# Laying every engine's instruction list a second time, by when each step can begin, in a four-layer fp32-accurate transformer kernel

## The reference

```
L0: mod = silu(c) @ w_adaln + b;  x += g1 * attention(modulate(ln(x)));  x += g2 * moe(modulate(ln(x)))   # 4 experts, top 2
L1: the same form with a plain MLP, and attention among the 16 heads of one token:
    softmax(einsum('nthd,ntkd->nthk', q * scale, k)), then einsum('nthk,ntkd->nthd', attn, v)
L2: attention over tokens, plain MLP
L3: U = qr(P).Q;  R = expm(skew(silu(cond) @ W.T + b));  x + ((x @ U) @ R - x @ U) @ U.T
```

## Time and profile before

| | |
|---|---|
| median of 3 runs | 1548.58 us (1545.59 to 1550.38) |
| profiled execution, its own time | 1545.17 us |
| its span, first to last instruction | 1543.1 us |
| mean granted TensorE clock | 0.952 of full |
| instructions | 30439 |
| busy: TensorE, VectorE, ScalarE, GpSimd | 1367.0, 950.9, 818.6, 397.8 us |
| DMA | 91.82 MB, mean 60 GB/s |

### The profile page before, as it was taken

The page is one execution under the profiler, slowest core; times in us unless marked ns, Lnnn a source line. Parts: engine busy times, 40 slices in busy tenths (PEclk is TensorE's granted clock), DMA queues, the critical chain, the costliest instruction groups (busy, mean ns, idle before and its releaser), DMA issues.

```text
span 1543.1 us, 30439 instructions
## 1 busy us (share of the span) xinstructions
PE 1367.0 (89%) x11841; PEld 822.0 (53%) x11841; DVE 950.9 (62%) x2315; ACT 818.6 (53%) x1597; POOL 397.8 (26%) x571
## 2 busy tenths in 40 slices
PE   4667999897999989999899988788899989998988
PEld 2333555563655545655466554455465556555655
DVE  5666877746567555555465555766777866656453
ACT  2555655657566424653345433675555665654542
POOL 1122232213233221222231322232332423321110
PEclk9887999998999999999999999899999999998998
DMA  5122234452213120321113122230000120000010
GB/s 154 48 65 92 83 102 136 149 158 86 65 43 104 38 76 8 75 80 62 51 24 96 44 75 83 51 67 13 17 9 5 36 74 13 5 7 13 1 39 31
DMA packets 76740, 91.82 MB, mean 60 GB/s; under 512 B 38989, under 2 KB 69814, under 8 KB 73270
## 3 DMA queue, kind: packets, MB, share of 16 engines
q1 hardware_dynamic: 74486, 87.52, 19.6%
q10 hardware_dynamic: 2112, 2.36, 0.5%
HBM read 73.22 MB, written 16.38 MB: 58 GB/s over the span
## 4 chain that ended last, share of the span: by engine, by line
PE 60%; DVE 13%; issue 10%; ACT 5%; DMA 5%; POOL 4%; SPq 2%; DVEq 0%; POOLq 0%; ACTq 0%
PE P L1346 27%; PE P L1506 4%; PE P L1508 4%; PE P L1507 4%; PE P L1475 3%; DVE NM L1776 3%; PE P L1466 2%; PE P L1373 2%; PE P L1442 2%; PE P L1523 1%; POOL N L2225 1%; PE P L1363 1%; POOL X L2210 1%; PE P L1517 1%; DVE AT L1908 1%
## 5 line engine op out<-in xcount | busy, mean ns | idle before, releaser
L1346 PE MATMUL P<-XT,W 128*128 128x512 f16 x1512 | 355.5, 387 | 6.1 <-DVE NM L1776 2.6
L2210 POOL TENSOR_TENSOR X<-X,TM 128x288 f32<-128x288 f32 x144 | 122.0, 847 | 660.3 <-DVE TM L1851 438.8
L1506 PE MATMUL P<-W,H 128*128 128x288 f16 x864 | 252.9, 293 | 1.1 <-DVE H L1845 1.0
L1507 PE MATMUL P<-W,H 128*128 128x288 f16 x864 | 252.4, 292 | 0.0
L1508 PE MATMUL P<-W,H 128*128 128x288 f16 x864 | 252.3, 292 | 0.0
L1346 PEld LDWEIGHTS P<-XT,W 128*128 128x128 f16 x1512 | 143.8, 99 | 180.5 <-issue 21.3
L2118 ACT ACTIVATE ARENA<-P 128x512 f32<-128x512 f32 x256 | 136.7, 596 | 122.7 <-PE P L1466 122.2
L2128 ACT ACTIVATE G<-P 128x512 f32<-128x512 f32 x216 | 128.4, 594 | 126.9 <-PE P L1346 115.8
L1776 DVE TENSOR_REDUCE NM<-P 128x2 f16<-128x512 f32 x256 | 159.8, 686 | 3.5 <-PE P L1451 2.9
L1845 DVE TENSOR_TENSOR H<-G,H 128x512 f16<-128x512 f32 x138 | 98.9, 719 | 82.0 <-ACT H L2129 81.5
L1346 PE MATMUL P<-WQ,XT 128*128 128x288 f16 x1008 | 143.6, 294 | 1.5 <-DVE NM L1776 0.9
(11 more groups left out here) (307 smaller groups left out, 2232.1 us busy)
## 6 DMA issues: line engine op xcount, KB each, us to landing
W<-scr_w SPq DMA_DIRECT2D x9, 1440.0 KB, 6.0
W<-scr_w SPq DMA_DIRECT2D x9, 1368.0 KB, 5.9
scr_w<-W SPq DMA_DIRECT2D x4, 1440.0 KB, 6.4
scr_w<-W SPq DMA_DIRECT2D x4, 1368.0 KB, 5.7
STG<-in_L_w SPq DMA_DIRECT2D x8, 576.0 KB, 4.3
STG<-in_L_w SPq DMA_DIRECT2D x9, 432.0 KB, 4.1
STG<-in_L_WT SPq DMA_DIRECT2D x11, 324.0 KB, 4.2
G<-scr_ada SPq DMA_DIRECT2D x24, 144.0 KB, 3.7
```

The source lines that it names most:

```text
L1346: ins = e.matmul(o, l, r, start=k == 0, stop=k == len(pairs_) - 1)
L1506: e.matmul(o, hi, W2[:, 2 * m, :], start=False, stop=False)
L1507: e.matmul(o, hi, W2[:, 2 * m + 1, :], start=False, stop=False)
L2210: e.tensor_tensor(X[:, t, :], X[:, t, :], TM[st["k"]][:, :], ALU.add).then_inc(st.sem)
```

## The change

The first pass plans as before, with other costs. Then `by_readiness` lays the five lists again. On each lane the steps are sorted into queues that keep their order: one queue for each semaphore, on SP one queue for everything, and on ScalarE one queue for all steps that need a function table. In each round every lane offers one head of a queue: of the heads whose dependences are all laid, the one that can begin first by the account (all that can begin within NEAR = 0.1 us of the time at which the lane is free count as equal, and the one that stood first in the old list is taken). The lane whose offer begins earliest gets its step laid. PSUM banks, buffers, engines and waits of each step stay as the first pass gave them.

The costs of the account change too, and two constants of the first pass.

```
-SLACK, BIAS = -0.68, 0.18
+NEAR = 0.1
+TABLES = dict(exps="exp", t_exp="exp", g_exp="exp", gelu="gelu", silu="silu")
+SLACK, BIAS = -0.6, 0.2
...
+def by_readiness(lanes):
+    queues, table = [], None
+    for lane in lanes:
+        some = {}
+        for k, st in enumerate(lane.steps):
+            st.index, st.end = k, None
+            name = "dma" if lane.name == "sp" else "table" if st.kind in TABLES else id(st.sem)
+            some.setdefault(name, deque()).append(st)
+        queues.append(list(some.values()))
+        lane.steps, lane.clock = [], 0.0
+    while True:
+        best = None
+        for lane, some in zip(lanes, queues):
+            mine = None
+            for qu in some:
+                if qu and all(x.end is not None for x in qu[0].deps):
+                    begin = max(lane.clock, max((x.end for x in qu[0].deps), default=0.0) + LAT)
+                    key = (begin if begin > lane.clock + NEAR else lane.clock, qu[0].index)
+                    if mine is None or key < mine[0]:
+                        mine = key, begin, qu
+            if mine and (best is None or mine[1] < best[0]):
+                best = mine[1], lane, mine[2]
+        if best is None:
+            return
+        begin, lane, qu = best
+        st = qu.popleft()
+        if st.kind in TABLES and TABLES[st.kind] != table:
+            table, begin = TABLES[st.kind], begin + TAB
+        lane.clock = begin + st.cost
+        st.end = lane.clock + st.tail
+        lane.steps.append(st)
...
+            st.cost, st.tail, st.deps = cost, st.end - lane.clock, [x for v in fields.values() if isinstance(v, (Step, list, tuple)) for x in flat(v) if isinstance(x, Step)]
...
-            return n * max(0.058, cols / 2240 * wide + 0.003)
+            return n * max(0.058, cols / 2230 * wide + 0.001)
...
         deal([loads, attends, ends_, tops, preps, bg, *(Line(rotated(k), 5) for k in range(2))])
+
+        by_readiness([pe, dve, act, pool, sp])
```

More of the change, by code:

```diff
@@ L1 @@
+from collections import deque
 from contextlib import ExitStack
@@ L362, in split_cols @@
                     else:
-                        x = do(act, "w_hi3", 0.2 + (b - a) * 0.00085, dst=dst, rows=96 if bias is None else 128, a=a, b=b, scale=s, i=i, src=ld, free=before)
+                        x = do(act, "w_hi3", 0.15 + (b - a) * 0.00085, dst=dst, rows=96 if bias is None else 128, a=a, b=b, scale=s, i=i, src=ld, free=before)
                         y = do(dve, "w_lo3", 0.1 + (b - a) * 0.0011, dst=dst, rows=32 if bias is None else 64, a=a, b=b, scale=s, i=i, src=ld, hi=x)
@@ L489, in layernorm @@
                 s = do(dve, "ln_stats", 0.45, w=w, n=n, t=t, x=XW[t], free=tok.get(("st", w)))
-                aggr.append(do(dve, "ln_aggr", 0.18, w=w, n=n, src=s, free=tok.get(("mv", w))))
+                aggr.append(do(dve, "ln_aggr", 0.13, w=w, n=n, src=s, free=tok.get(("mv", w))))
             tok["st", w] = list(aggr)
@@ L511, in layernorm @@
             before = TR[2 * b] + TR[2 * b + 1]
-            f = copy("full", 1.1 + BIAS, 1.15, L=L, b=b, sc=sc, sh=sh, mixed=mixed, i=i, js=(j, j2), src=m, cols=cols, free=ff)
+            f = copy("full", 1.42 + BIAS, 1.42, L=L, b=b, sc=sc, sh=sh, mixed=mixed, i=i, js=(j, j2), src=m, cols=cols, free=ff)
             rP.free[j], rP.free[j2] = [f], [f]
             yield [f]
-            hi = copy("m_hi", 0.95 + BIAS, 0.75, b=b, i=i, src=f, free=before)
+            hi = copy("m_hi", 0.9 + BIAS, 0.68, b=b, i=i, src=f, free=before)
             yield [hi]
-            lane, cost = sooner([hi], (pool, 2.5), (dve, 1.35))
+            lane, cost = sooner([hi], (pool, 3.0), (dve, 1.6))
             lo = do(lane, "m_lo", cost, raises=f"m_lo_{lane.name}", incs=3 if lane is pool else 1, b=b, i=i, src=hi, free=before)
@@ L536, in turned @@
                 yield [m]
-                v = copy("tq" if name == "q" else "tk", 1.03 + BIAS, 1.22, u=u, g=g, j=j, src=m, free=free)
+                v = copy("tq" if name == "q" else "tk", 0.97 + BIAS, 1.14, u=u, g=g, j=j, src=m, free=free)
                 rP.free[j] = [v]
@@ L623, in heads @@
                 yield [m]
-                a = do(act, name + "_hi", 0.66, n=n, j=j, src=m, free=last[n])
+                a = do(act, name + "_hi", 0.56, n=n, j=j, src=m, free=last[n])
                 yield [a]
-                d = do(dve, name + "_lo", 0.46, n=n, j=j, src=m, hi=a, free=last[n])
+                d = do(dve, name + "_lo", 0.42, n=n, j=j, src=m, hi=a, free=last[n])
                 rP.free[j] = [a, d]
@@ L638, in heads @@
                 yield [m]
[L639 removed]
+                v = copy("qt" if name == "q" else "kt", 0.93 + BIAS, 0.62, u=u, n=n, j=j, src=m, free=(qt_rd if name == "q" else kt_rd)[u])
                 rP.free[j] = [v]
@@ L702, in product @@
             def product(c, i, ready, j, jf, js, jsf):
-                m = do(pe, "t_av", 1.05, u=u, c=c, i=i, j=j, js=js, e=ready, free=[jf, jsf], v=tok["v", b])
+                m = do(pe, "t_av", 0.55, u=u, c=c, i=i, j=j, js=js, e=ready, free=[jf, jsf], v=tok["v", b])
                 rE1.free[i] = [m]
@@ L718, in attend_tokens @@
                     for n, jj in enumerate((j, j2)):
-                        ready.append(do(act, "t_exp", 0.6, j=jj, i=i, n=n, src=m, free=ef))
+                        ready.append(do(act, "t_exp", 0.5, j=jj, i=i, n=n, src=m, free=ef))
                         rP.free[jj] = [ready[-1]]
@@ L795, in exps @@
                 for par, j in enumerate(js):
-                    got.append(do(act, "exps", 0.6, j=j, s=s, h=(2 * c + par) % 4, src=m, free=ef))
+                    got.append(do(act, "exps", 0.5, j=j, s=s, h=(2 * c + par) % 4, src=m, free=ef))
                     rP.free[j] = [got[-1]]
@@ L800, in av @@
             def av(g, s, j, jf, ready):
-                m = do(pe, "av", 1.0, u=u, g=g, s=s, j=j, e=ready, free=jf, v=tok["v", b])
+                m = do(pe, "av", 0.58, u=u, g=g, s=s, j=j, e=ready, free=jf, v=tok["v", b])
                 rE.free[s] = [m]
@@ L805, in evict @@
             def evict(g, j, m):
-                v = copy("ot", 0.6 + BIAS, 0.69, g=g, j=j, src=m, free=ot_rd[0])
+                v = copy("ot", 0.51 + BIAS, 0.63, g=g, j=j, src=m, free=ot_rd[0])
                 rP.free[j] = [v]
@@ L889, in finish @@
                 if L == 1:
-                    m = do(pe, "t_proj", mm_cost(4, C, 4), n=n, j=j, o=tok["o", 1, b], w=tok["wp", 1], free=pf)
+                    m = do(pe, "t_proj", 1.25, n=n, j=j, o=tok["o", 1, b], w=tok["wp", 1], free=pf)
                     ms_.append(m)
@@ L897, in finish @@
                 k, _, tf = rTM.take()
-                v = do(dve, "proj_gate", 0.47, L=L, j=j, k=k, u=u, src=m, rows=rows, free=tf)
+                v = do(dve, "proj_gate", 0.41, L=L, j=j, k=k, u=u, src=m, rows=rows, free=tf)
                 rP.free[j] = [v]
@@ L944, in low @@
                 m, gi, a = lows.pop(0)
-                lane, cost = sooner([a], (pool, 1.3), (dve, 0.8))
+                lane, cost = sooner([a], (pool, 1.3), (dve, 0.7))
                 d = do(lane, "h_lo", cost, raises=f"h_lo_{lane.name}", m=m, gi=gi, src=a, free=h_rd[0])
@@ L1064, in householder @@
                 _, c, pf = rP.take()
-                m = do(pe, "hh_mm", mm_cost(1, C - j, 4) + 0.1, c=j, j=c, src=last, free=pf)
+                m = do(pe, "hh_mm", 0.1 + (C - j) * 0.0017, c=j, j=c, src=last, free=pf)
                 yield
-                a = do(act, "hh_row", 0.55, incs=2, c=j, j=c, src=m, free=last if j else None)
+                a = do(act, "hh_row", 0.95, incs=2, c=j, j=c, src=m, free=last if j else None)
                 rP.free[c] = [a]
@@ L1147, in rotated @@
                 _, j, pf = rP.take()
-                m = do(pe, "m_mm", mm_cost(1, C, 4), b=b, j=j, cur=cur, e=e, u=tok["U"], free=pf)
+                m = do(pe, "m_mm", 0.6, b=b, j=j, cur=cur, e=e, u=tok["U"], free=pf)
                 yield [m]
```

40 lines of the change are left out of this document (20 added, 20 removed).

## The result

The changed kernel takes 1470.39 us (1467.42 to 1474.97, 4 runs) against 1549.48 (1545.59 to 1551.41, 4 runs): a ratio of 0.9495, 95% interval 0.9459 to 0.9531, 79 us less. The forecast was 35 us less and a range that ended at 1484; the way was right, the size less than half.

What follows compares the result with a forecast made beforehand. TensorE, busy 1367.0 of 1543.1 us, was taken as the bound; −17 − 17 − 4 + 12 − 9 = −35 gave a span of 1508, and with run offsets 1514 us, range 1490 to 1536 (1484 to 1556 with rivals).

Steps and rivals of the forecast that it cites:

- B: TensorE's waits after 160 us other than Householder ones, 85.0 us: one in five filled, −17 us, bounds 0 and −42.
- E: New TensorE waits where the plan is wrong about what is ready: +12 us, bounds 0 and +38.
- D: TensorE's time at the lower clock, costing 54.4 us, shrinks in proportion to idle time: −9 us, bounds 0 and −25.
- A: TensorE's waits before the Householder product `hh_mm`, 34.3 us: half filled, −17 us, bounds 0 and −34.
- C: TensorE's idle time before 160 us without the first load, 38.9 us: one in ten filled, −4 us, bounds 0 and −15.
- part (1): Account of `by_readiness`: ready TensorE groups pass a waiting product; GpSimd's gain matters only through those who wait for it.
- More is filled: Rival: reordering sees nearly every TensorE hole and fills more, −75 us, giving 1474 us; chance 0.10.
- Nothing comes of it: Rival: old TensorE holes go and new ones come because the plan's account errs, 1544 to 1553 us; chance 0.12.
- TensorE isn't the bound: Rival: TensorE's matmul busy time misleads, so filling its idle time brings nothing; chance 0.01, counted within no gain.
- Hand-overs: Rival: fillers delay hand-overs between engines in attention, mainly before 160 us, by 1 us each: 1580 us; chance 0.12.
- Collisions: Rival: VectorE and GpSimd instructions lock each other out more often, 0.88 us a time; 60 give 1567 us; chance 0.05.
- The late background chain: Way to fail: the new first pass lays the background chain 20 us later, leaving the kernel's tail without filler.

## Why the prediction was right in direction and wrong in size

*The bound, and what can be won: right.* The gain is idle time of TensorE and clock, to within 4 us of the span's difference. Term by term, against the span (B and E can't be told apart in a trace; D is the fall of busy time; all in us):

| | forecast | changed kernel | second laying alone | TensorE alone free, old costs |
|---|---|---|---|---|
| first load | 0 | +4.1 | −1.2 | +1.7 |
| A, Householder waits | −17 | −22.2 | −31.1 | −25.3 |
| B + E, other idle time after 160 us | −5 | −28.0 | −12.7 | −5.7 |
| C, the start | −4 | −8.7 | −0.8 | −3.5 |
| D, the clock | −9 | −15.1 | −22.0 | −3.7 |
| sum | −35 | −69.9 | −67.8 | −36.5 |

*TensorE's filling (A, B, C with E): the size was that of TensorE alone.* The sum gave −35 us from the holes that TensorE could fill by itself. With TensorE alone free on the old costs the kernel got 36 us faster. B with E and C are as forecast in that run; that the whole fits is luck in part: A was too small by 8 us and D too large by 5.

*The step that failed is the one on the other engines* in part (1): that what GpSimd gains "matters only through those who wait for it", after which neither it nor VectorE or ScalarE got a term. They were treated as cover (VectorE 62% busy, ScalarE 53%) and their lists priced at nothing. But each was a fixed list too, which stands before a step that isn't ready with a ready one behind it on which TensorE's next group hangs, as at 1023.40. Freed without TensorE they gave 21 to 24 us, and on top of TensorE's filling 34 (1511 to 1477), 13.0 of idle time and 18.3 of busy time in the spans. That is nearly all of the second laying's gain beyond the forecast (73 − 35 = 38). The rows to read it from were there: the waits of VectorE, of which the prediction used none.

*Terms B and E, −17 and +12, net too small:* the two new waits named above are 8.2 and 6.1 us, and the idle time after 160 us that is not Householder's fell by 28.0 us. With all engines free the Householder wait fell to 3.2 us even on the old costs. A wrong price costs less after a second laying than before it, as the table of the orders shows.

*D, the clock: mechanism right, rule of proportion not.* The lower level gave back 18.9 us by the stretches (15.1 of busy time) against 9, and the stretches left still cost half of 71.1, 35.5 us. The prediction took 54.4/158.2 = 0.34 us per us of idle time removed. In the changed kernel busy time fell by 0.28 us for each, but by 0.11 with TensorE alone free (3.7 for 32.8) and by 0.48 with the second laying alone (22.0 for 45.8). How much idle time goes does not tell how much clock comes back; what does is not shown here.

*The costs.* That the account's fp32 prices are far below the measured durations was right. That this is the harmless side is neither shown nor refuted once both passes run: 11 us one way in one pair, 8 the other way in the next. In the first pass alone the right prices are better by 14 us, within the scatter. "I take 0" for the new costs held in the sum: second laying alone 1477 and 1472, all of the change 1470 and 1471. For the first pass alone it would have been far off, 53 us.

*The rivals.* More is filled: its sum was −75 against the span, the measured one −69.9, but it put all of it on TensorE filling its own holes (A −34 against −22.2; B with E −14 against −28.0), and TensorE alone was worth 36. That it named the time is luck in part. Nothing comes of it: refuted; with it that TensorE isn't the bound, since filling its idle time did shorten the kernel. Hand-overs: refuted, the first stage does more work in its 160 us (938 matmuls against 902). Collisions: VectorE's busy time rose by 5.5 us of 950.9, but 22 instructions moved to it and 26 went from GpSimd; with the second laying alone, where the counts of both are those of before, it rose by 1.5. Refuted as a cost of weight. A fixed number of instructions, forecast, was nearly so (30371 against 30439): the choices between engines came out anew. The late background chain: the opposite.

*What stays open.* Which of the new costs makes a first pass slower when it is used alone. All three orders with new costs (1588, 1602, 1624) lie above all three with old ones (1549, 1566, 1573). Part of the 52 us is that the kernel before was a low point by 16 to 24 us; what is left, some 30 us against its neighbours, has no single cause shown. A version faster than the changed kernel was measured once, at 1459 us, but its neighbour at 1479 says that it is one fortunate order and not a better plan.

## What to carry to other kernels

Where lists are carried out in order, look at every engine's waits before you price a new order, not only those of the busiest: an engine that is idle for a third of the time still delays the bound if it stands before the wrong step. Here a list pass that lets ready steps go ahead was worth more than accurate prices, and it made the time less sensitive to them. A forecast that meets the total can still have two terms wrong that cancel: compare it term by term. Before you credit an edit of a planner with one per cent, nudge a constant that should not matter and see how far the time moves.
